# Attention of a gated cross-attention block: units of 256 queries in place of 512, and another division of the eight PSUM banks

## The reference

```python
x = x + tanh(g_xattn) * attention(layernorm(x), ctx, ctx)   # q,k,v: 256 -> 8 heads of 4; softmax over 1601 keys; Wo: 32 -> 256
y = layernorm(x)
scores = softmax(y @ router_w + router_b)                   # 2048 x 8
G, idx = top_k(scores.T, 512)
for e in range(8):                                          # relu(y[idx] @ w1 + b1) @ w2 + b2, weighted by G, added at idx
    ...
x = x + tanh(g_ffn) * that
```

## Time and profile before

| | |
|---|---|
| median of the runs | 684.34 us (3 runs, 683.17 to 684.45) |
| the profiled execution | 682.07 us |
| its span, first to last instruction | 680.3 us |
| mean granted clock of TensorE | 0.911 of full speed |
| busy: TensorE, VectorE, ScalarE, GpSimd | 539.6, 476.8, 395.4, 160.1 us |

### The profile page before, as it was taken

How to read it: one execution, slowest core, us unless ns; L and a number is a source line. 1 busy time by engine, 2 the same in 40 slices (tenths; PEclk the granted TensorE clock), 3 DMA queues, 4 the chain that set the end, 5 groups by cost and what they waited for, 6 DMA issues and landing times.

```text
span 680.3 us, 10063 instructions
## 1 busy us (share of the span) xinstructions
PE 539.6 (79%) x3452; PEld 278.4 (41%) x3452; DVE 476.8 (70%) x952; ACT 395.4 (58%) x748; POOL 160.1 (24%) x161
## 2 busy tenths in 40 slices
PE   4766798888989889888898843015999999999991
PEld 3322122112322223222222120004988988988991
DVE  3788877889788897988883035883686786776531
ACT  2563378777777777777778921002555566466551
POOL 3022212002020020730000001005063464364333
PEclk9976599999999999999999975555999999999997
DMA  7500000000000000000000014002164563564222
GB/s 255 192 1 0 1 0 1 2 1 1 0 33 32 1 1 0 32 32 1 1 32 31 1 46 139 0 0 62 32 159 119 105 173 99 125 155 102 54 33 31
DMA packets 23330, 35.45 MB, mean 52 GB/s; under 512 B 3411, under 2 KB 15988, under 8 KB 23156
## 3 DMA queue, kind: packets, MB, share of 16 engines
q1 hardware_dynamic: 17140, 26.45, 11.9%
q0 software_dynamic: 6144, 8.39, 7.3%
HBM read 26.45 MB, written 8.39 MB: 51 GB/s over the span
## 4 chain that ended last, share of the span: by engine, by line
PE 54%; DVE 19%; ACT 13%; issue 7%; POOL 1%; DMA 0%; DVEq 0%; POOLq 0%; ACTq 0%
PE ps L1295 11%; PE ps L1199 11%; PE ps L1400 10%; PE ps L1407 10%; ACT probs L615 8%; DVE mquart L821 6%; PE ps L1182 3%; DVE ge L995 3%; PE ps L1145 2%; ACT eo L704 1%; PE ps L1222 1%; PE ps L1234 1%; ACT hf L695 1%; DVE tokl L1072 1%; DVE h1l L1086 1%
## 5 line engine op out<-in xcount | busy, mean ns | idle before, releaser
L821 DVE TENSOR_REDUCE mquart<-ps 128x2 f32<-128x802 f32 x256 | 246.2, 989 | 48.3 <-PE ps L1182 43.7
L615 ACT ACTIVATE probs<-ps 128x512 f32<-128x512 f32 (+1 forms) x416 | 224.1, 600 | 81.6 <-PE ps L1295 80.1
L1295 PE MATMUL ps<-qfull,kpad 64*128 64x512 bf16 (+1 forms) x416 | 129.5, 390 | 28.3 <-ACT probs L615 28.2
L1182 PE MATMUL ps<-kpad,qrows 64*128 64x401 bf16 x512 | 128.1, 355 | 14.7 <-DVE mquart L821 13.2
L1199 PE MATMUL ps<-probs,vp 128*32 128x512 f32 (+1 forms) x832 | 112.1, 611 | 5.6 <-ACT probs L615 4.1
L1295 PEld LDWEIGHTS ps<-qfull,kpad 64*128 64x128 bf16 (+1 forms) x416 | 29.4, 95 | 172.1 <-ACT probs L615 156.2
L1086 DVE TENSOR_TENSOR h1l<-hf,h1h 128x512 fp32r<-128x512 f32 x64 | 44.5, 695 | 62.1 <-ACT hf L695 62.1
L694 ACT ACTIVATE h1h<-ps,b1T 128x512 fp32r<-128x512 f32 x64 | 43.9, 686 | 60.4 <-PE ps L1400 60.3
L1407 PE MATMUL ps<-w2h,h1h 128*128 128x256 f32 x256 | 73.8, 288 | 3.3 <-DVE h1l L1086 3.3
L1407 PE MATMUL ps<-w2l,h1h 128*128 128x256 f32 x256 | 72.4, 283 | 0.0
L1407 PE MATMUL ps<-w2h,h1l 128*128 128x256 f32 x256 | 72.3, 282 | 0.0
(11 more groups left out here) (167 smaller groups left out, 668.0 us busy)
## 6 DMA issues: line engine op xcount, KB each, us to landing
w1raw<-in_L_ffn_w SPq DMA_DIRECT2D x16, 512.0 KB, 4.2
w2raw<-in_L_ffn_w SPq DMA_DIRECT2D x16, 512.0 KB, 4.7
xs<-in_x SPq DMA_DIRECT2D x4, 512.0 KB, 7.9
out<-xs SPq DMA_DIRECT2D x4, 512.0 KB, 3.1
x_rows<-x SPq DMA_DIRECT2D x4, 512.0 KB, 2.6
ctx_sb<-in_ctx SPq DMA_DIRECT2D x3, 512.0 KB, 6.3
b2b<-in_L_ffn_b SPq DMA_DIRECT2D x1, 1024.0 KB, 12.3
toks<-x_rows,idx_get POOLq DMA_INDIRECT x32, 2.8
```

The source lines that it names most:

```text
L615: nc.scalar.activation(probs[0:w, par, ORDER[hh], :], ps[0:w, score_bank(kt, hh, last_unit), :], ACT.Exp, scale=float(SCALE)).then_inc(s_e ...
L821: nc.vector.tensor_reduce(mquart[:, n // HG, n % HG // 2, :, kq], ps[:, b:b + 2, 0:MAXW], AX.X, ALU.max).then_inc(s_mr, 1)
L1182: last = mm(ps[:, 2 + 2 * (j % 2) + b, 0:MAXW], qrows[head_rows(hh), g, a:a + P], kpad[head_rows(hh), HG * g + hh, lo:lo + MAXW], start=Tr ...
L1295: mm(ps[0:w, score_bank(kt, hh, last_unit), :], kpad[head_rows(ORDER[hh]), HG * g + ORDER[hh], P * kt:P * kt + w], qfull[head_rows(ORDER[h ...
```

## The change

- **Units.** A unit is 256 queries of a group (`UQ = 2`, `UW = 256`): 16 units with 16 max tiles each. The number of max tiles (256) and of exponentials (416, each over 512 columns) stays. One exponential now covers two heads x 256 queries: `scores` is two matmuls of 256 columns into the two halves of a bank, both in one band. A value step is four matmuls of 256 columns.
- **PSUM.** Banks 0, 1, 2 are a ring for what ScalarE reads (`next_act`), banks 3 and 4, 5 and 6 a ring of two for what VectorE reads (`next_dve`), bank 7 holds the values. Side work takes the next place of the ring of the engine that reads it. The bank `JOB` of its own is gone.
- **Order on TensorE.** `probs` holds 6 steps in place of 2. Values are issued two steps at a time, at every second step, for the tiles two and three back; the last three tiles of a unit are issued at step 1 of the next unit.
- **Lead.** Max tiles run four steps further ahead (`LEAD = 4`), so 20 of them stand before the first score matmul, where 36 did.
- **`kpad`** has two variants for each group in place of four, so it takes 8 instructions in place of 16 for each group.
- **Before the attention** VectorE takes half of the transposed context (`take_ctx`), the first query projection comes after the keys, and `pad_k1` and `take_v` of group 1 run one block behind.
- **Layernorm.** Its last step (subtract the mean, times the inverse deviation) moves from VectorE to GpSimd (`ln1_apply`, `ln2_apply`), for all but the first chunk's first and the last chunk's second layernorm. GpSimd's first weights come behind all of it.
- **Router.** It is eight small products whose result has the rows in partitions, so the transposing of the logits and ScalarE's copy go. `wo` is one job of four matmuls, with one `residual` over 1024 columns.

The core of the diff:

```diff
-ORDER = (0, 2, 1, 3)
-HALVES = CT * (HG // 2) * QUARTERS
+UQ = 2
+UW = UQ * P
+PARTS = CT // UQ
+PER_CHUNK = NG * PARTS
+UNITS = NC * PER_CHUNK
+TILES = UQ * 2 * QUARTERS
+LEAD = 4
+PROBS = 6
...
-        PV, JOB = 6, 7
+        PV, JOB = 7, 2
...
+        def tiles_by(u, i):
+
+            return min(TILES * UNITS, TILES * (u + 1) + TILES * (i + 1 + 2 * LEAD) // (2 * NKT))
...
+        O_THIS, O_LAST, BACK_AT, WO_AT = (2, 4), (0, 4), (0, 7), (0, 10)
+        XN_AT, Q_AT = ((0, 9), (0, 11)), ((1, 3), (1, 6))
+        X2_AT, ROUTER_AT = ((2, 6), (2, 8)), (2, 11)
...
+            def next_act(reader):
+
+                n = len(act_readers)
+                if n >= 3:
+                    pe.wait_ge(*act_readers[n - 3])
+                act_readers.append(reader)
+                return act_bank(n)
+
+            def next_dve(reader):
+
+                n = len(dve_readers)
+                if n >= 2:
+                    pe.wait_ge(*dve_readers[n - 2])
+                dve_readers.append(reader)
+                return dve_bank(n)
...
+            def scores(u, kt, p):
+
+                c, g, h, r = unit(u)
+                w = kt_rows(kt)
+                bank = next_act((s_ex, 2 * (NKT * u + kt) + p + 1))
+                for b in range(2):
+                    last = mm(ps[0:w, bank, UW * b:UW * b + UW], kpad[band(p), g, b, P * kt:P * kt + w],
+                              qfull[band(p), g, UW * h:UW * h + UW], start=True, stop=True)
+                last.then_inc(s_sc, 1)
...
+            for u in range(UNITS):
+                c, g, h, r = unit(u)
+                pe.wait_ge(s_qf, u + 1)
+                for kt in range(NKT):
+                    for p in range(2):
+                        i = 2 * kt + p
+                        scores(u, kt, p)
+                        for n in range(tiles_by(u, i - 1), tiles_by(u, i)):
+                            max_tile(n)
+                        if p == 1 and kt == 1 and u > 0:
+                            for k in range(NKT - 3, NKT):
+                                pv(u - 1, k)
+                        if p == 1 and kt % 2 == 1 and kt > 1:
+                            pv(u, kt - 3)
+                            pv(u, kt - 2)
+                    if kt == PLACE and u + 1 < UNITS:
+                        place_max(u + 1)
```

More of the change, by code:

```diff
@@ L931, in chunk @@
-            def chunk(i, first, last):
-                for g in range(NG):
-                    u = 2 * i + g
-                    ahead = (1 - g) if last else 2
-                    for kt in range(NKT):
-                        halves = halves_of(kt, ahead)
-                        if kt == PLACE + 1 and ahead:
-                            q_full(u + 1, i + g, (g + 1) % 2)
-                        for at in range(3):
-                            if at < len(halves):
-                                du, j = halves[at]
-                                max_half(u + du, j)
-                                if (du, j) == (1, HALVES - 1):
-                                    max_parts(u + 1)
-                            beside(i, g, u, (kt, at), first, last)
@@ L1180, in max_scores @@
                 for b in range(2):
[L1181 to L1183 removed]
+                    last = mm(ps[:, bank + b, 0:MAXW], qrows[band(b), g, q:q + P], kpad[band(b), g, a, lo:lo + MAXW], start=True, stop=True)
                 last.then_inc(s_mm, 1)
@@ L1187, in place_max @@
                 pe.wait_ge(s_mp, u + 1)
-                for t in range(CT):
-                    last = mm(job[:, P * t:P * t + P], mparts[:, t, :, :].rearrange("p h r -> p (h r)"), ident_bf[:, :], start=True, stop=True)
+                bank = next_dve((s_qf, u + 1))
+                for t in range(UQ):
+                    last = mm(ps[:, bank, P * t:P * t + P], mparts[:, t, :, :].rearrange("p h r -> p (h r)"), ident_bf[:, :], start=True, stop=True)
                 last.then_inc(s_mpl, 1)
-            def pv(step, c, g, kt):
+            def scores(u, kt, p):
+                c, g, h, r = unit(u)
@@ L1229, in transpose_x2, with router @@
                 last.then_inc(s_X, 1)
-            def router(c):
+            def router(c, bank):
                 pe.wait_ge(s_Xt, KD * (c + 1))
-                for k in range(KD):
-                    last = mm(job[0:E, :], rw_sb[:, k, :], x2T[:, k, :], start=(k == 0), stop=(k == KD - 1))
+                for t in range(CT):
+                    for k in range(KD):
+                        last = mm(ps[:, bank, E * t:E * t + E], x2T[:, k, P * t:P * t + P], rw_sb[:, k, :], start=(k == 0), stop=(k == KD - 1))
@@ L1350, in _ @@
                 transpose_x2(c, k, k)
[L1351 to L1352 removed]
+            router(c, 2)
             pe.wait_ge(s_score, 1)
```

597 lines of the change are left out of this document (285 added, 312 removed).

## The result

The changed kernel takes 687.78 us (median of 20 runs) beside 683.43 for the kernel before on the same chip. The ratio is 1.0069, with a 95% interval of 1.0045 to 1.0093: 0.7% slower, where 645.7 was forecast. Two of its 20 executions (694.9 and 915.9 us) fell into a slower state and are left out of the ratio. The profiled execution took 687.83 us with a span of 685.7.

The account below looks back on a forecast made before the run. The prediction saw a chain over two banks, no engine, as the bound. A 57.5, B 279 and C 19 end the attention at 355.5 in place of 393.2; with 1 us saved behind it, 645.7 us was forecast, range 619 to 671.

Parts of the forecast that it names:

- A: Stretch up to the first exponential, with 20 max tiles ahead of the scores: forecast to end at 57.5 us, before 74.5.
- C: Stretch of exponentials alone, from the last max tile's end to the last exponential's end: forecast 19 us, before 33.9.
- What TensorE needs: TensorE's work per unit beside the attention: 16.1 us, with 0.57 us per value step, near VectorE's 16.8.
- The rival on the number of instructions: Value steps on TensorE stay at 1.0 us because instruction count sets them: kernel 690 us, chance 0.06.
- B: Stretch where max tiles run beside exponentials, 236 tiles: forecast 279 us, 1.18 per tile; before 284.8 us.
- What is late next: Stalls when TensorE's values and side jobs outlast VectorE's ring: 8.8 us per chunk, some 27 over B.
- floor of 248 us: VectorE's bare work in B: 236 max tiles, 214.3 us, plus 34 us of side work; 1.05 per tile.
- Three banks hide the value block from ScalarE: ScalarE's ring in the attention: its waits cost nothing, since ScalarE has 10% of cover.
- The ring of VectorE: VectorE's ring holds two tiles, 1.8 us; TensorE, in order, is at most that far ahead when it turns to values.
- The wait moves and the pace stays: In B, in-order TensorE waits for two rings in turn: 1.27 per tile, B 300, kernel 667 us; chance 0.17.
- VectorE at its floor: In B TensorE keeps ahead and stalls of 27 us shrink to 5: kernel 624 us; chance 0.15.
- GpSimd: GpSimd instructions hold VectorE's mparts in B, half of 15 at 1.2 us each: 9 us, kernel 655; chance 0.08.

Follow-up runs that it names:

- e1_singles: The changed kernel with one value step issued after every step's scores, in place of two together every second step: 663.78 us, ratio to before 0.9700.
- e12: The changed kernel with VectorE's one-bank side jobs (placing of maxima, transposed outputs, router) moved into ScalarE's ring of three banks: 673.93 us, 0.9878.
- e11: e1_singles with VectorE's one-bank side jobs (placing of maxima, transposed outputs, router) moved into ScalarE's ring of three banks: 648.20 us, 0.9482.
- e6: e1_singles with each query projection and each wo product issued in two pieces, and wo moved from step 10 to 12: 663.99 us, 0.9711.
- e2: The changed kernel with the second half of each query projection of chunks 1 to 3 left out: 688.97 us, 1.0086.
- e7_fill: e1_singles with ten extra bf16 matmuls, never read, ahead of the placing of the maxima in 14 units: 661.5 us, 0.9671.

## Why the prediction was wrong, by its own steps

- **What bounds the kernel** was read rightly: a chain over two banks, no engine. **A** (57.5, measured 57.8) held. **C** (19, measured 22.0) did not quite: its pairs take 2.40 us where I had ScalarE's 1.95, so the 3 us are the failed step below once more.
- **What TensorE needs** held too: two value steps take 1.00 us, 0.50 each, under the 0.57 that I took. The rival on the number of instructions is refuted, though its figures (B 321, end of the attention at 400, kernel 690) are all but the measured ones (320.0, 399.9, 687.8). That is luck: it needed a value step of 1.0 us.
- **"What is late next" is the step that failed.** I priced the stalls of B at 27 us, 8.8 a chunk. By the same floor of 248 us and 4 us for the first clock they are 68. Two sentences of it were wrong.
  - *"Three banks hide the value block from ScalarE; I cost the ring's waits at nothing."* I compared ScalarE's work with its capacity over a unit (10% of cover) and not what three banks hold when a block starts. TensorE begins the block only when the fourth score pair has its bank, by then one exponential is gone, and block and way are 1.43 us. Splitting the pairs gave 24.0 us back (e1_singles): the mis-sized term.
  - *The ring of VectorE.* I counted how long TensorE is away from it, never what a side job in it does. It holds a slot of two, TensorE waits for it ahead of the job, and the scores wait too. I had put 0.9 for `wo` with the placing once a chunk; small jobs in that ring cost 13.9 us (e12) and 15.6 (e11), some 3 of the 15.6 by way of the clock.
- With both mended B is 282.7 (forecast 279) and the kernel takes 648.2 (forecast 645.7). The forecast fits a kernel in which the two assumptions are true; the agreement to 1% is partly luck, since e11's B also holds what the clock and the projections cost.
- **The clock.** I allowed 4 us at the start and nothing later. Four stretches at 1.2 GHz cost 4 to 6 us in the profiled execution, which is as much as the kernel's whole loss. Without them it would be level with before, not faster, as its executions at the highest clock are (684.2 us at 0.916).
- **The rivals.** "The wait moves and the pace stays" had the right mechanism, in-order TensorE between two rings, and 0.17; I gave it 1.27 a tile by likeness to before, without working out the loop, and it is 1.356. The steady loop (17.2 us for 16 tiles) is 1.08 a tile; what lies beyond is placings, unit starts and side jobs, of which little is hidden. "VectorE at its floor" was far off.
- **GpSimd** did what its rival said, at a small price: 4 of the 15 times in B an instruction on `mparts` took 1.0 to 1.2 us in place of 0.2, some 3.5 us in all, each beside a GpSimd addition or subtraction of 1.15 to 1.26 us. The first case, from the changed kernel's timeline:

```profile
97.57 1.15 POOL L351 TENSOR_TENSOR qrows<-t,c 128x512 bf16<-128x512 f32 x1 [1.31 <-ACT c L585]
97.75 1.02 DVE L875 CAST mparts<-nmax 128x8 bf16<-128x8 f32 x1
```

**What stays open.** Units with side jobs still take 19.3 to 21.8 us in e11's middle chunks against 16.15 without; the longest holds 4.0 us of projections and is 5.7 us longer, so it looks as if nothing of them is hidden. Neither cutting the jobs (e6) nor halving a projection (e2) told cleanly why. And what the clock would do with the router of before was not tried.

## What to carry to other kernels

When one in-order engine feeds two others, write out the loop instant by instant: what each ring holds at the moment a block starts, against the block plus the way to the consumer's first instruction. Spare capacity over a longer stretch hides nothing by itself. Issue the feeder's own long work in the smallest pieces that don't hold a bank longer, and keep small jobs out of the ring that is already the slower one's: both moves left the work unchanged and took 6% off the changed kernel.

## What the hardware showed that I had not expected

- TensorE's clock fell to 1.2 GHz in the middle of busy work: from 157.6 to 161.0 us it was busy 2.58 of 3.40 us and its longest pause was 0.80, and the next 3.4 us ran at half clock. Ahead of the stretch from 212.2 it was busy 3.08 of 3.40 us, and ahead of e11's from 192.7 all the time (3.40 of 3.40), both times with a router job of 16 matmuls of 8 columns. The kernel before, with TensorE 33.90 of 40 us busy, kept full clock from 84 us to the end of the attention. The Trainium skill, "TensorE: Matmul & The Clock Gate", section "A second HAM failure mode: psum-queue depth-cycling", describes such swinging for a TensorE that goes round PSUM banks with short pauses between groups; the falls at the placings agree with it, at 1.0 to 1.5 us for each stretch; those behind a router job come without such pauses.
- Leaving out 6 us of matmuls did not make the kernel faster (e2_half_q), and adding some 15 us of them did not make it slower (e7_fill).
- At 1.2 GHz TensorE can stay for long though it is busy: 11.22 of 12 us in the window of e12, with no rise for 24 us.
- A cast with one operand in SBUF, 128x8, took 1.02 us beside a GpSimd instruction, against 0.19 without one; no reduction over 802 columns took more than 1.00 us. The Trainium skill, "SBUF — State Buffer", section "Who interferes with whom", counts casts among the VectorE instructions that can lock the ports shared with GpSimd, and reductions not; the rows agree. In the forecast I had named only its rule on two operands.
